# A mixture-of-experts and attention layer on one core: both gate and up products of a tile ahead of all its down matmuls

## The reference

```
xn = layernorm(x)
s  = attention(xn)          # a second layernorm inside, causal softmax, o_proj, + xn
g  = silu(ffn(xn))
out = x + s * g

ffn(xn):  gates = softmax(xn @ router_w.T); the two best of E=8 experts, renormalised
          routed = sum over the two experts e of g_e * (silu(xn@wg[e]) * (xn@wu[e])) @ wd[e]   # H=352
          shared = (silu(xn@sg) * (xn@su)) @ sd                                              # width 704
          return routed + shared
```

## Time and profile before

| | |
|---|---|
| median of 3 runs (lowest, highest) | 1158.92 us (1158.82, 1160.46) |
| the profiled execution, its own time | 1158.34 us |
| its span, from the first to the last instruction | 1156.6 us |
| PE busy | 1132.1 us, 98% |
| DVE busy | 570.5 us, 49% |
| ACT busy | 473.5 us, 41% |
| POOL busy | 423.4 us, 37% |
| share of the DMA engines' busy time, in tenths | 9 in the slice from 87 to 116 us, 5 in that from 376 to 405 us |
| granted PE clock, mean | 0.998 |

### The profile page before, as it was taken

One profiled execution on the slowest core, in us unless ns is written; L12 is line 12 of the kernel. 1 busy time (PEld: TensorE's weight loads), 2 busy tenths in 40 slices (PEclk: granted clock), 3 DMA queues, 4 the chain that ended last, 5 costly groups with the idle time before them and its releaser, 6 DMA issues. The chain is left out here.

```text
span 1156.6 us, 21228 instructions
## 1 busy us (share of the span) xinstructions
PE 1132.1 (98%) x6598; PEld 627.3 (54%) x6599; DVE 570.5 (49%) x1236; ACT 473.5 (41%) x859; POOL 423.4 (37%) x656
## 2 busy tenths in 40 slices
PE   8899999999999999999999999998999999999997
PEld 5555555555555555555555555554454444444454
DVE  6866667677468322211221122111377467467467
ACT  5544444444332223322332233224645545654643
POOL 1363333332200122222222222212764764764663
PEclk9999999999999999999999999999999999999999
DMA  9889999989633589989898878776767668766355
GB/s 288 232 190 219 232 233 236 202 220 231 158 71 77 117 170 209 207 198 209 193 203 191 185 173 182 179 169 163 152 163 186 157 160 184 166 161 182 114 150 126
DMA packets 365004, 209.31 MB, mean 181 GB/s; under 512 B 304309, under 2 KB 314817, under 8 KB 364937
## 3 DMA queue, kind: packets, MB, share of 16 engines
q1 hardware_dynamic: 354104, 172.76, 64.7%
q0 software_dynamic: 10800, 35.69, 12.2%
q10 hardware_dynamic: 32, 0.02, 0.0%
HBM read 89.44 MB, written 46.01 MB: 117 GB/s over the span
## 5 line engine op out<-in xcount | busy, mean ns | idle before, releaser
L708 PE MATMUL pair<-arena 128*128 (+2 forms) x3240 | 506.2, 313 | 0.2 <-issue 0.2
L708 PEld LDWEIGHTS pair<-arena 128*128 128x128 f16 x3240 | 316.1, 98 | 182.6 <-issue 0.9
L1629 DVE SCALAR_TENSOR_TENSOR arena<-pair,slot_unit,arena 128x352 f32<-128x352 f32 x71 | 41.4, 583 | 268.8 <-ACT arena L1519 220.3
L715 PE MATMUL bank<-arena 128*128 x639 | 149.3, 379 | 1.3 <-DMA arena<-arena 1.3
L1519 ACT ACTIVATE arena<-pair,slot_unit 128x352 f32<-128x352 f32 x71 | 39.4, 555 | 205.5 <-PE pair L708 172.1
L1238 POOL COPY arena<-token_of 128x1 uint32 (+1 forms) x71 | 13.0, 183 | 271.3 <-issue 103.3
L715 PEld LDWEIGHTS bank<-arena 128*128 128x128 f16 x639 | 62.5, 98 | 67.7 <-issue 1.8
L1910 PE MATMUL pair<-arena 128*128 128x512 f16 (+3 forms) x576 | 97.5, 326 | 0.6 <-ACT arena L1979 0.6
L1923 PE MATMUL bank<-arena 128*128 128x512 f16 x411 | 93.4, 379 | 0.0
L1240 POOL DMA_INDIRECT arena<-xn_rows,arena x71 | 71.4, 1005 | 55.7 <-POOL arena L1238 54.1
L1895 PE MATMUL bank<-arena 128*128 128x512 f16 x384 | 86.0, 379 | 1.6 <-PEq L1058 1.6
(11 more groups left out here) (205 smaller groups left out, 1356.4 us busy)
## 6 DMA issues: line engine op xcount, KB each, us to landing
slot_rows<-arena SPq DMA_DIRECT2D x71, 256.0 KB
arena<-in_L_attn_x_dram SPq DMA_DIRECT2D x64, 256.0 KB, 3.6
xn_rows<-arena SPq DMA_DIRECT2D x32, 260.0 KB, 2.5
shared_rows<-arena SPq DMA_DIRECT2D x32, 256.0 KB
arena<-shared_rows SPq DMA_DIRECT2D x32, 256.0 KB
out_dram<-arena SPq DMA_DIRECT2D x31, 256.0 KB, 2.8
arena<-in_L_ffn_wg_dram SPq DMA_DIRECT2D x32, 176.0 KB, 3.1
arena<-in_L_ffn_wu_dram SPq DMA_DIRECT2D x32, 176.0 KB, 3.4
```

What stands on the lines that cost most here:

```text
L708: last = pe.matmul(bank[:, 0:width], xt[:, a, c, :], weights(c, b, col, width), start=(c == 0 and i == 0), stop=(c == KC - 1 and i == 2))
L715: last = pe.matmul(bank[:, :], ht[:, a, c, :], weights(c, b), start=(start and c == 0 and i == 0), stop=(stop and c == HC - 1 and i == 2))
L1629: v.scalar_tensor_tensor(sbuf[u], u_banks[u][:, 0:H], slot_unit[u][:, 1:2], sbuf[u], ALU.mult, ALU.mult).then_inc(slot_h_ready, 1)
```

## The change

The change moves calls in PE's list alone. No other engine's list is touched, and every matmul, operand and bank stays. In each step both `unit_in` come first, and behind them both `unit_down` of the tile before, 17 matmuls in one row. At the passage to the slot tiles `slot_in` of tiles 0 and 1 come first and the last two `unit_down` behind them. `ranks`, `turn_bias`, `late_router` and `hot_product` keep their places in the text of the loop, so those with b = 0 now stand between the first and the second `unit_in`.

```diff
                             unit_in(n, b)
-                            if s > 0:
-                                if s == 1:
-                                    fold_banks_free(pe, 2)
-                                    pe.wait_ge(shared_lo, IN_SPLITS + 2 * (b + 1))
-                                unit_down(n - 2, b)
+                            if s == 1 and b == 1:
+                                fold_banks_free(pe, 2)
+                                pe.wait_ge(shared_lo, IN_SPLITS + 4)
+                            if s > 0 and b == 1:
+                                unit_down(n - 3, 0)
+                                unit_down(n - 2, 1)
                             if n == 2:
                                 turn_bias(pe)
...
                     for j in range(2):
                         slot_in(j, j, 0)
+                    for j in range(2):
                         unit_down(2 * NT - 2 + j, j)
```

## The result

The changed kernel takes **1162.95 us** (median of 7 runs, 1162.52 to 1165.44), the kernel before, on the same chip, 1157.9 (7 runs, 1156.42 to 1160.46). The ratio is **1.0044, interval 1.0032 to 1.0055**: slower by 5.05 us. The forecast was 1159.6 with a range up to 1161.9, and no measurable difference as the likeliest. It was wrong: the change was given +0.65 us and cost 5.05.

A forecast was written before the change was run, and what follows sets the result against it. PE, busy 98% of the span, was taken as the bound. Even pauses -0.65 and one-hot steps +1.30 gave +0.65 on 1158.34, so 1158.99; with 0.58 for the median, 1159.6 us, range 1157.4 to 1161.9.

The forecast's parts named there:

- The one-hot steps, +1.30: Steps 28 to 30: the even down no longer lies under DVE's work, so the stage ends 1.30 us later.
- The early chain, taken at 0: Pauses at the stage's start: the odd down waits for a transfer PE doesn't time, so nothing is gained, 0.
- The clock in step 28: Rival: step 28's pause grows from 1.52 to 2.8 us and the clock falls there, +1.7 us, 1161.3; chance 0.20.
- Even pauses, -0.65: Two short waits ahead of even downs, 0.24 and 0.41 us, go because turned rows get 3.57 us more; -0.65 us.
- SP, 0: SP's even turning waits longer for PE; mostly absorbed, 0.9 us gets through in step 15; taken as 0, bounds 0 and +1.7.
- SP's new wait shows: Rival: late loads reach odd downs of steps 7, 10, 16 or 19, once or twice; 1161 to 1163 us, chance 0.08.
- Odd pauses, 0: Three pauses ahead of odd downs, 4.6 us: PE stands nowhere in their chain; taken as 0, bounds 0 to -4.6.
- PE does time the early chain: Rival: the three odd and the early even pauses go, 4.6 + 1.6 us, giving 1153.4 us; chance 0.07.
- Passage, 0: Passage to the slot tiles: 4.4 us are left for turning slot tile 1's rows; taken as 0, bounds 0 and +1.2.
- Matmuls, 0: All steps: number, sizes and banks of matmuls stay, and so does the step's 10.87 us; taken as 0.
- What I said would show it: Predicted profile signs: even downs never pause PE, first slot tile 0.6 us later, clock 1.00 around 354 us.

The follow-up runs named there:

- e11: The kernel before with the new order in steps 1 to 5 alone; 1160.85 us, ratio 1.0017.
- e13: The changed kernel with the passage to the slot tiles in the old order; 1164.1 us, ratio 1.0044.
- e2: The changed kernel with step 1 alone in the old order; 1164.46 us, ratio 1.0042, five runs.
- e4: The changed kernel with steps 1 to 5 in the old order; 1163.87 us, ratio 1.0042, five runs.
- e10: The kernel before with the new order in steps 28, 29 and 30 alone; 1160.98 us, ratio 1.0015.
- after: The profiled execution of the changed kernel itself, with no further edit; 1162.52 us.
- e3: The changed kernel with 14 extra unused matmuls between the two downs of step 1, filling its pause; 1161.9 us, ratio 1.0029.
- e9: The changed kernel with both pauses filled, 14 extra matmuls in step 1 and 11 in step 28; 1163.24 us, ratio 1.0035.
- e8: The changed kernel with 11 extra unused matmuls ahead of one-hot product 1 of step 28, filling its pause; 1160.83 us, ratio 1.0017.
- e5: The kernel before with the new order in steps 6 to 27 alone; 1159.6 us, ratio 1.0002.
- e1: The changed kernel with one-hot steps 28, 29 and 30 in the old order; 1161.29 us, ratio 1.0018.
- e12: The kernel before with only the passage to the slot tiles in the new order; 1159.05 us, ratio 0.9997.
- e7: The kernel before, old order, with the one-hot products of b = 0 moved behind both downs of their step; 1156.26 us, ratio 0.9981.

## Why the prediction was wrong, point by point

*The one-hot steps, +1.30: right.* The old and new rows of the last table are 1.30 us apart, and the reason was the right one: product 1 stands as it did against DVE, the later two pauses end 12.7 us apart, and with the products behind the downs the loss is gone.

*The early chain, taken at 0, and the clock behind it: this is the step that failed.* Of the pauses at the start the prediction says "Those at the start don't", because the odd down "waits for a transfer that PE doesn't time; PE merely arrives there earlier and waits for both". In step 1 both halves of that came out otherwise. The odd down starts 20.3 to 22.0 us after the stage's start with the new order, and 19.3 to 19.7 with the old one, so PE's order does move what it waits for, and makes it later. And the pause, 1.6 to 3.1 us before, is 3.8 to 4.4, behind which the clock fell in all seven unfilled profiles, for 3.4 or 6.8 us, which costs 1.7 or 3.4; with the old order it fell in four of nine, for 3.4. I had priced the clock in step 28 alone. The early steps alone cost 1.0017, or 2 us (e11), of which 2.1 are clock by the estimate, and of the 5.2 us of e13 3.2 are clock.

*The clock in step 28: a rival, with too small a chance.* Against it I put that pauses of 1.7 and 1.66 us left the clock at 0.998, said that it decides "between 1.7 and 2.8 us", and gave it 0.20. It fell in 3 of the 6 unfilled profiles with the new order (e2, e4, e10), for 1.4 to 1.7 us, at 2.48 or 2.49 us of visible idle time, and not in the other three (after, e3, e13) at the same 2.48 or 2.49. One profile can't show that. That the pause brings the fall is shown for step 1 by e3 and e9, which only fill it; for step 28 it rests on e2, e4 and e10 and on e8's mean clock.

*Even pauses, -0.65: gone, but seldom there.* The two of the middle did go. But the other profiles with the old order there have less of them or none, so as a gain over the kernel's usual execution they were worth less: one profile was taken for all.

*SP, 0: mis-sized.* SP waits for PE's even down 25 times and 93.5 us instead of 10 times and 20.1, and odd downs now pause where they hadn't: 0.15 at 138, 0.59 at 204 and 0.39 at 237 by the starts of groups, 1.1 us in all. That is the rival "SP's new wait shows", in small coins. It came in step 15's neighbourhood, where I had found the tightest place, but I had rounded 0.9 us of lateness down to nothing. Between the two profiles of the change the middle is +0.65 and not -0.65. e5's 1.0002 agrees with a middle that neither wins nor loses, but its interval would also hold -0.65.

*A wait that I didn't price.* Second gate and up now comes 1.30 us earlier, and its banks may still be DVE's: PE waited for DVE there for 1.45 us in e4, 0.37 in e1 and 0.30 in e3, and for 0.28 in step 1 of the changed kernel. In the kernel before there is no such wait.

*Odd pauses, 0: wrong in sign.* They take 5.9 us instead of 4.6. The pause of 103.46 is still there (1.41 at 104.55), that of 1.2 at 78.88 is gone, and the one of step 1 has grown by 2.1. The rival that "PE does time the early chain" was right in that PE's order matters there and wrong in what it does: no profile with the new order has the early pauses gone, and e11 is slower.

*Passage, 0: right* as far as e12 tells (0.9997, 0.9987 to 1.0008). *Matmuls, 0*: nothing in the profiles speaks against it.

*What I said would show it.* "Even downs never pause PE" didn't hold, 1.31 us stand at 52.30. The first slot tile starts 3.0 us later and not 0.6. "The granted clock stays at 1.00 around 354 us" held in the profile after; the other profiles say that it was luck. "If PE waits for turned rows at a place that is new" was named as what makes me wrong, and it came.

**What stays open.** Why the odd turning of step 1 takes longer with the new order. Why e2 and e4 are no faster than the whole change, when e11 alone costs 1.0017: both have only five runs, and the difference is no larger than the intervals together allow. Why e9 has such a rest. In the eight profiles with the new one-hot steps and the products in their old place the slot tiles take 399.1 to 401.4 us, 400.2 in the mean; in the other ten 399.0 to 400.2, 399.4 in the mean. The longer ones have short waits for turned rows, up to 1.6 us together in e8; whether that hangs on the change isn't settled. The +1.5 of e10's rest may hold some of it.

## What to carry to other kernels

Work that PE does under another engine's wait must stay ahead of that wait: moved behind it, it costs its whole length (1.30 us here), and where the wait is moved behind work that is ready, its idle time goes too, as with the one-hot products (1.8 us of steps 28 to 31 in e7). A pause that grows from under 2 us to 2.5 or 4 can cost more than its growth, because the clock may halve for 3.4 us or more behind it, and that can be a matter of chance: read the mean granted clock of all runs, not of the one that has the profile. A short pause seen in one profile may not be in the others. And a new wait of the queue engine isn't free because most of it is absorbed; the steps with the least slack have to be summed one by one.

## What the runs showed of the hardware

From 36 to 400 us the clock fell in or right behind these pauses of PE: 2.30 us (e7, at 102.31), 2.48 or 2.49 (step 28 of e2, e4 and e10), 2.56 (e9) and 2.89 to 4.38 (step 1 of eleven profiles). It stayed full at 2.48 or 2.49 us in step 28 of after, e3 and e13, and at all pauses of 1.8 us and less. It fell to 0.50 and came back after 3.4 or 6.8 us. In e11, one of the latter, PE was still idle for 1.1 us of the first 3.4 and busy in all of the second (60.40 to 63.80). From the issue of step 1's odd transposing DMA to the start of its reader 3.4 to 5.3 us went by: 3.4 to 4.4 with the old order of step 1, and 4.8 to 5.3 with the new one, filled or not.
